# Attention weights made the stationary operand of "weights times values", with four tokens in column tiles, and the hand-over between four stages of a one-core layer rescheduled

## The reference

```python
q = (x @ wq.T + bq).reshape(B, S, 32, 16)      # k and v alike
scores = einsum('bshd,bstd->bsht', q, k) / 4   # 32 x 32 for each token
probs = softmax(scores, axis=-1)
context = einsum('bsht,bstd->bshd', probs, v).reshape(B, S, 512)
x = layernorm(x + context)
# feed-forward: w1, w2 (1376 x 512) and w3 (512 x 1376) are first quantised to the 16 values
# of NF4 in blocks of 64 (scaled by the block's largest magnitude) and dequantised
h = silu(x @ dq(w1).T) * (x @ dq(w2).T)
x = layernorm(x + h @ dq(w3).T)
```

## Time and profile before

| | |
|---|---|
| median of 3 runs | 812.72 us (812.71 to 813.48) |
| profiled execution, its own time | 811.45 us |
| span in the profile | 809.6 us |
| mean granted clock of TensorE | 0.847 |
| busy: PE, VectorE (DVE), ScalarE (ACT), POOL | 737.6, 630.4, 484.5, 102.6 us |
| DMA | 118.45 MB, mean 146 GB/s |

### The profile page before, as it was taken

The page is one execution under the profiler, slowest core; times in us unless marked ns, Lnnn a source line. Parts: engine busy times, 40 slices in busy tenths (PEclk is TensorE's granted clock), DMA queues, the critical chain, the costliest instruction groups (busy, mean ns, idle before and its releaser), DMA issues.

```text
span 809.6 us, 14305 instructions
## 1 busy us (share of the span) xinstructions
PE 737.6 (91%) x5688; PEld 629.3 (78%) x5688; DVE 630.4 (78%) x876; ACT 484.5 (60%) x650; POOL 102.6 (13%) x97
## 2 busy tenths in 40 slices
PE   5899999765899999999699999997999999899993
PEld 4778788654899999999587888885888888688761
DVE  2799999579888898987488998877787575965286
ACT  3688989384654636556554778674674546663124
POOL 2011101103000001010011111020111110100022
PEclk9999999975555655555699999998999999999995
DMA  9954444999987794963606260210415101340257
GB/s 221 232 159 156 148 155 157 257 243 259 234 214 189 226 262 135 278 157 133 232 1 203 85 210 26 81 54 26 141 30 171 45 4 35 118 148 12 104 157 155
DMA packets 89522, 118.45 MB, mean 146 GB/s; under 512 B 24784, under 2 KB 70864, under 8 KB 86512
## 3 DMA queue, kind: packets, MB, share of 16 engines
q1 hardware_dynamic: 88320, 115.44, 50.7%
q10 hardware_dynamic: 1136, 2.10, 1.2%
HBM read 76.42 MB, written 38.86 MB: 142 GB/s over the span
## 4 chain that ended last, share of the span: by engine, by line
PE 63%; DVE 12%; issue 9%; ACT 6%; DMA 4%; SPq 3%; POOL 1%; POOLq 0%; DVEq 0%; ACTq 0%
PE ps_p L1013 9%; PE ps_s L914 9%; PE ps_s L916 9%; PE ps_s L915 9%; PE ps_p L914 7%; PE ps_p L916 6%; PE ps_p L915 6%; DVE nf_acc L1136 4%; ACT nf_y L747 3%; PE ps_s L1000 3%; DMA qk_parts<-qk_p 2%; PE ps_t L952 1%; PE ps_t L938 1%; DMA k_st<-qk_parts 1%; SPq L408 1%
## 5 line engine op out<-in xcount | busy, mean ns | idle before, releaser
L1136 DVE SCALAR_TENSOR_TENSOR nf_acc<-nf_y,nf_acc 128x1024 f32<-128x1024 f32 (+4 forms) x266 | 303.3, 1140 | 32.5 <-ACT nf_y L747 23.6
L747 ACT ACTIVATE nf_y<-nf_w,bound_b 128x1024 f32<-128x1024 f32 (+4 forms) x285 | 288.9, 1047 | 9.7 <-DVE nf_acc L1136 4.0
L1013 PE MATMUL ps_p<-probT,v_bd 128*68 128x32 f32 x1024 | 125.6, 301 | 3.3 <-DVE probT L1185 3.3
L1013 PEld LDWEIGHTS ps_p<-probT,v_bd 128*68 128x68 f32 x1024 | 122.9, 211 | 4.4 <-issue 3.2
L1295 DVE TENSOR_TENSOR silu<-silu,ps_s 128x512 f32<-128x512 f32 (+1 forms) x44 | 30.2, 686 | 91.4 <-PE ps_s L916 91.2
L914 PE MATMUL ps_p<-x_hl,w_hl 128*128 128x512 f32 x192 | 78.8, 410 | 16.0 <-DVE qk_r L1160 10.3
L891 ACT ACTIVATE silu<-ps_s 128x512 f32<-128x512 f32 (+1 forms) x44 | 26.2, 596 | 95.6 <-PE ps_s L916 95.6
L668 POOL TENSOR_TENSOR nf_w<-nf_w,nf_rec 128x1024 f32<-128x1024 f32 (+4 forms) x19 | 39.7, 2089 | 335.4 <-DVE nf_rec L1120 335.4
L914 PE MATMUL ps_s<-x_hl,f_ha 128*128 128x512 f32 x192 | 76.1, 396 | 5.7 <-issue 5.7
L916 PE MATMUL ps_p<-x_hl,w_hl 128*128 128x512 f32 x192 | 76.7, 399 | 0.0
L915 PE MATMUL ps_p<-x_hl,w_hl 128*128 128x512 f32 x192 | 76.5, 399 | 0.0
(11 more groups left out here) (105 smaller groups left out, 1246.6 us busy)
## 6 DMA issues: line engine op xcount, KB each, us to landing
x_hl<-x_parts SPq DMA_DIRECT2D x10, 2048.0 KB, 8.9
qk_parts<-qk_p SPq DMA_DIRECT2D x64, 204.0 KB, 2.5
q_st<-qk_parts SPq DMA_DIRECT2D x48, 272.0 KB, 6.8
k_st<-qk_parts SPq DMA_DIRECT2D x48, 272.0 KB, 7.6
x_parts<-x_st SPq DMA_DIRECT2D x16, 512.0 KB, 3.8
nf_w<-in_L_ffn_w SPq DMA_DIRECT2D x24, 256.0 KB, 3.0
dequantised<-nf_acc SPq DMA_DIRECT2D x10, 512.0 KB, 4.4
v_blocks<-v_t SPq DMA_DIRECT2D x16, 256.0 KB, 3.0
```

The source lines that it names most:

```text
L747: act.activation(nf_y[0:p, at % NY, 0:w], nf_w[0:p, u % 2, 0:w], ACT.Identity, bias=bound_b[0:p, i:i + 1], scale=STEEP).then_inc(s_ny, 1)
L1013: t = pe.matmul(ps_p[0:MV, (G + 3) % NPV, i * H:(i + 1) * H], v_bd[hb % 2][:, :, g * GI + i], probT[:, G % 2, i], start=True, stop=True)
L1136: dve.scalar_tensor_tensor(out=acc, in0=y, scalar=float(NF4[i + 1]), in1=acc, op0=ALU.min, op1=ALU.max).then_inc(s_nacc, 1)
```

## The change

1. `values`: the softmax weights of one token (32 columns) are stationary, its block-diagonal values (68 columns) move. Four tokens are put side by side in the four column tiles of 32 PSUM partitions; the result of 16 such matmuls lies in [128, 4 x 68]. New: `evacuate` (ScalarE copies it to `ctmp`, three buffers) and `back` (four PE transposes bring it to [68, 512] in another PSUM bank), then `context` as before, a group later. Turns, moments and normalisation of a block come one group later.
2. First seam: the stack loads of half-block 0 are spread over three later slots, the value loads over a fourth; the last three slots of the projections have 1, 0, 0 levels instead of 2, 2, 2.
3. Second seam: x1 of the first block is loaded within the last group; the tail's turns use two more banks and another order of units; the last `back` and `context` come after the first gate and up chains.
4. Third and fourth seam: units are ordered first "w", both "t", other "w"; the levels per step change.

```diff
+        first = len(js) if g == 0 else 1
+        UNITS += [("w", g, j) for j in js[:first]] + [("t", g, t) for t in range(2)] + [("w", g, j) for j in js[first:]]
...
+    FIRST_STACKS = [FIRST_LOAD + 1 + 2 * k for k in range(3)]
+    FIRST_VALUES = FIRST_LOAD + 7
     LV_P = [1, 1, 1, 1, 1, 1, 1, 1, 2, 2, 2, 2] * NBK
+    LV_P[-3:] = [1, 0, 0]
...
-        LV_A[8 * b + 10:8 * b + 13] = [1, 1, 1]
+        LV_A[8 * b + 11:8 * b + 14] = [1, 1, 1]
...
-    LV_F = [(1, 2)] * 2 + [(1, 1)] * 2 + [(1, 2)] + [(2, 2)] * (FIRST_OF[2] - 5) + [(3, 4)] * 4 + [(3, 3)] * 2
+    LV_F = [(1, 2)] * 2 + [(1, 1)] * 2 + [(1, 0), (1, 2)] + [(2, 3)] * 20 + [(2, 2)] * 13
...
+    LATE = {8 * b + 8 + k: 8 * b + 14 + k // 2 for b in range(NBK - 1) for k in range(4)}
     for G in range(GG):
-        CONTEXT_AT.setdefault(max(G + 3, LATE.get(G, 0)), []).append(G)
+        CONTEXT_AT.setdefault(max(G + 4, LATE.get(G, 0)), []).append(G)
+        BACK_AT.setdefault(G + 4 if G % 8 == 2 and G > 8 else G + 3, []).append(G)
...
+    TAIL_1 = [("f", u, s) for u in (W_UNITS[0], T_UNITS[0]) for s in range(2)]
+    TAIL_2 = [("f", u, s) for u in (T_UNITS[1], W_UNITS[1]) for s in range(2)]
...
+    TAIL_S = (TAIL_1 + TAIL_2)[2:6]
+    def bank_of(n):
+        if n < NPT:
+            return n % 4
+        if TURNS[n] in TAIL_S:
+            return 2 + TAIL_S.index(TURNS[n]) % 2
+        return n % 2
...
+        ctmp = sb("ctmp", [P, NCT, 4 * MV], F32, att)
...
                     parts_stored(sp, 2 * KC)
-                    load_stacks(sp, 0)
+                if tau in FIRST_STACKS:
+                    load_stacks(sp, 0, [FIRST_STACKS.index(tau)])
+                if tau == FIRST_VALUES:
...
+                if G == GG - 1:
+                    load_x1(0)
...
+            def evacuate(G):
+                if G == 0:
+                    values_stored(act, KC * NBK)
+                act.wait_ge(s_pv, G + 1)
+                wait(act, s_back, G - NCT + 1)
+                act.activation(ctmp[:, G % NCT], ps_p[:, G % 2, 0:4 * MV], ACT.Copy).then_inc(s_evac, 1)
...
-                wait(pe, s_ctx, G - NPV + 1)
+                wait(pe, s_evac, G - 1)
                 for i in range(GI):
-                    t = pe.matmul(ps_p[0:MV, (G + 3) % NPV, i * H:(i + 1) * H], v_bd[hb % 2][:, :, g * GI + i],
-                                  probT[:, G % 2, i], start=True, stop=True)
+                    a, j = divmod(i, 4)
+                    t = pe.matmul(ps_p[32 * j:32 * j + 32, G % 2, a * MV:(a + 1) * MV], probT[:, G % 2, i],
+                                  v_bd[hb % 2][:, :, g * GI + i], start=True, stop=True)
                 t.then_inc(s_pv, 1)
+
+            def back(G):
+                pe.wait_ge(s_evac, G + 1)
+                wait(pe, s_ctx, G - 1)
+                for a in range(4):
+                    t = pe.transpose(ps_p[0:MV, 2 + G % 2, P * a:P * a + P], ctmp[:, G % NCT, a * MV:(a + 1) * MV],
+                                     ident[:])
+                t.then_inc(s_back, 1)
...
             for s in range(NS):
                 gate_up(s)
+                if s == 0:
+                    back(GG - 1)
```

More of the change, by code:

```diff
@@ L155, in layer_kernel @@
     HEADS = [range(0, 7), range(7, 14), range(14, 21), range(21, 28), range(28, 32)]
[L156 removed]
+    CT_AT, XT_AT, MOMENTS_AT, NORM_AT = {}, {}, {}, {}
     for b in range(NBK - 1):
         for k in range(len(HEADS)):
[L159 to L161 removed]
+            CT_AT.setdefault(8 * b + 11 + k // 2, []).append(("ct", b, k))
+        MOMENTS_AT[8 * b + 13] = b
+        NORM_AT[8 * b + 14] = b
         for c in range(KC):
[L163 to L166 removed]
+            XT_AT.setdefault(8 * b + 15 + c // 2, []).append(("xt", b, c))
+    BACK_AT, CONTEXT_AT = {}, {}
+    LATE = {8 * b + 8 + k: 8 * b + 14 + k // 2 for b in range(NBK - 1) for k in range(4)}
     for G in range(GG):
[L168 to L169 removed]
+        CONTEXT_AT.setdefault(max(G + 4, LATE.get(G, 0)), []).append(G)
+        BACK_AT.setdefault(G + 4 if G % 8 == 2 and G > 8 else G + 3, []).append(G)
+    for G in range(GG + 1):
         TURNS += CT_AT.get(G, []) + XT_AT.get(G, [])
@@ L208, in layer_kernel @@
     TURN = {key: n for n, key in enumerate(TURNS)}
+    TAIL_S = (TAIL_1 + TAIL_2)[2:6]
[5 more added lines that the diff above has]
+        return n % 2
+    EARLIER = {key: max((m for m in range(n) if bank_of(m) == bank_of(n)), default=-1) for key, n in TURN.items()}
     HIGH = {key: n for n, key in enumerate(k for k in TURNS if k[0] != "ct")}
@@ L273, in layer_kernel @@
         f3_la = sb("f3_la", [P, NJG, E], F32R)
+        x1_hl_0 = sb("x1_hl0", [P, 2, KC, BK], F32R)
         f3_ha = sb("f3_ha", [P, NJG, E], F32R)
         f1_ha = sb("f1_ha", [P, 2, KC, NJG * P], F32R)
-        x1_hl = [sb(f"x1_hl{i}", [P, 2, KC, BK], F32R) for i in range(2)]
+        x1_hl = (x1_hl_0, sb("x1_hl1", [P, 2, KC, BK], F32R))
         hid_hl = sb("hid_hl", [P, 2, 2, BK], F32R)
@@ L321, in layer_kernel @@
         s_pv = sem("s_pv")
+        s_evac = sem("s_evac")
+        s_back = sem("s_back")
         s_ctx = sem("s_ctx")
@@ L400, in down_over, with load_stacks @@
                 eng.wait_ge(s_down, step + 1 - n)
-        def load_stacks(eng, hb):
-            for b in range(3):
+        def load_stacks(eng, hb, which=range(3)):
+            for b in which:
                 for i, terms in enumerate((Q_TERMS, K_TERMS)):
@@ L424, in turn_bank @@
         def turn_bank(key):
[L425 to L428, removed]
+            n = bank_of(TURN[key])
+            return (ps_t, ps_s)[n // 2][:, n % 2]
         def turn_shape(key):
@@ L522, in load_v, with store_x1, load_x1 @@
                                  ).then_inc(s_ldv[hb % 2], 16)
+            def store_x1(key):
+                _, b, c = key
+                low_done(sp, key)
+                sp.dma_start(x1_d[b, :, :, c], x1_st[:, c % 2].bitcast(F32)).then_inc(s_stx[c % 2], 16)
+            def load_x1(n):
+                b = ORDER[n][1]
+                if n == 0:
+                    sp.wait_ge(s_pv, GG - NG)
+                elif n == 1:
+                    sp.wait_ge(s_score, GG)
+                else:
+                    sp.wait_ge(s_up, LAST_STEP[max(k for k in range(n) if ORDER[k][1] == (b + 2) % NBK)] + 1)
+                x1_stored(sp, b)
+                sp.dma_start(x1_hl[b % 2][:].bitcast(F32), x1_d[b]).then_inc(s_ldx[b % 2], 16)
             for q in range(2):
@@ L599, in _ @@
                         reload(u)
+                if G == GG - 1:
+                    load_x1(0)
                 for key in XT_AT.get(G, []):
[L601 to L612, removed]
+                    store_x1(key)
+            for key in XT_AT.get(GG, []):
+                store_x1(key)
             def store_out(n, q):
@@ L861, in _ @@
                     context(at)
+                if G >= 3:
+                    evacuate(G - 3)
                 steep(LV_A[G] // 2)
@@ L868, in _ @@
                 steep(LV_A[G] - LV_A[G] // 2)
+            context(GG - 4)
+            evacuate(GG - 3)
+            for key in XT_AT.get(GG, []) + TAIL_1:
+                high(key)
+            evacuate(GG - 2)
             context(GG - 3)
-            for key in TAIL_1:
-                high(key)
-            context(GG - 2)
             steep(LV_T[0])
@@ L875, in _ @@
                 high(key)
-            context(GG - 1)
+            evacuate(GG - 1)
+            context(GG - 2)
             steep(LV_T[1])
@@ L891, in _ @@
                 act.activation(silu[0:rows, s % 2], ps_s[0:rows, 0], ACT.Silu).then_inc(s_silu, 1)
+                if s == 0:
+                    context(GG - 1)
                 steep(LV_F[s][0])
@@ L918, in turn @@
             def turn(key):
[L919 to L923, removed]
+                if EARLIER[key] >= 0:
+                    low_done(pe, TURNS[EARLIER[key]])
+                if key in TAIL_S[:2]:
+                    pe.wait_ge(s_ssub, GG)
                 kind, k, c = key
@@ L1078, in _ @@
                     values(G - 2)
+                for at in BACK_AT.get(G, []):
+                    back(at)
                 for key in XT_AT.get(G, []):
@@ L1081, in _ @@
             values(GG - 2)
-            for key in TAIL_1:
+            for key in XT_AT.get(GG, []) + TAIL_1:
                 turn(key)
+            back(GG - 3)
             values(GG - 1)
@@ L1086, in _ @@
                 turn(key)
+            back(GG - 2)
             pe.wait_ge(s_minus_i, 1)
```

21 lines of the change are left out of this document (8 added, 13 removed).

## The result

| | before | after |
|---|---|---|
| median, us | 813.1 (4 runs, 812.71 to 813.76) | 834.05 (4 runs, 831.39 to 836.3) |
| profiled execution: time / span | 811.45 / 809.6 | 834.1 / 832.3 |
| VectorE busy / ScalarE busy | 630.4 / 484.5 | 681.6 / 508.1 |

The ratio is 1.0256 [1.0224, 1.0287]: 21 us slower, where 26 us faster was predicted.

A forecast was written before the change was run, and what follows sets the result against it. TensorE and the VectorE-ScalarE loop were taken as level, the real losses as TensorE's idle seams. Terms -11.5 - 2.2 - 2.5 - 13.0 + 3 = -26.2 took 811.45 to 785.3, plus 1.3 for the median: 786 us; 8 in 10: 777 to 803.

The forecast's parts named there:

- The step that failed: Attention, steady state: TensorE's group falls to 4.1 us, under the VectorE-ScalarE loop, so little shows: -2.2 us.
- the 4.79: Attention: us a plain group takes in the VectorE-ScalarE loop of shift, exp, pass and lifts, read from the profile before.
- the range that I gave for TensorE's group: Attention: TensorE's group of scores, new product and transposes was put at 4.1 us, between 3.2 and 4.9.
- the sum: Whole kernel: all terms together, -26.2 us, giving 786 us; chance of 780 to 790 us 0.50.
- The product's 1.94 us: Attention, values: a token's second pass overlaps only the next token's first, so 16 x 121 ns a group.
- The lower bound of 1.0: Attention, values: with four column tiles wholly abreast the product takes 3.89/4 = 1.0 us a group.
- tiles in series: Rival, attention values: column tiles don't overlap, 813 us or up to about 905; chance 0.05 near no change, 0.08 clearly slower.
- ScalarE's evacuation: Attention: the added copy takes some 0.4 us a group (0.3 to 0.57), hidden in 1.56 us idle before exp.
- First seam, -11.5: Projections to attention: spread loads remove the 10.3 us store wait and group 4 starts earlier; -11.5 us, bounds 6 and 15.
- Second seam, -2.5: Attention to feed-forward: earlier x1 load and two more banks for the turns; -2.5 us, bounds 0 and -5.
- Third, fourth and the lifts, -13.0 + 3 = -10: Feed-forward: reordered units and fewer late lifts remove idle stretches, -13.0 us; extra lifts in steps 6 to 25 cost +3.
- the VectorE-bound rival: Rival, feed-forward steps 6 to 25: VectorE becomes the bound, +12 us in place of +3, 795 us; chance 0.20.

The follow-up runs named there:

- e1: The changed kernel with the old weights-times-values product, context read and order of turns, so the seams alone: 798.23 us, 0.9814 to the kernel before.
- e6: e1 with the values' rows padded to 272 bytes and three value buffers: 802.71 us, 0.9897 to the kernel before.
- e11: The changed kernel with 272-byte rows, without evacuations and transposes back, in the old order of turns: 796.31 us, 0.9798 to the kernel before.
- e8: e5 (272 bytes) with the stores of the first two x1 tiles issued ahead of the twelve stack loads: 800.86 us, 0.9854 to the kernel before.
- e5: The whole changed kernel with values' rows padded to 272 or 260 bytes and three value buffers: 804.56 us (272), 804.79 us (260).
- e3: The changed kernel with each product reading 68 consecutive numbers of the values' tile, not 68 standing 256 bytes apart: 803.12 us, 0.9879 to the kernel before.
- e9: The kernel before with the first seam alone, five lifts moved to the feed-forward: 809.28 us, 0.9959 to the kernel before.

## Why the prediction was wrong, step by step

**The step that failed** is in the attention: "TensorE's group becomes 1.28 + 1.94 + 0.88 = 4.1 ... under the 4.79 of the VectorE-ScalarE loop ... -2.2". The group did become short, and TensorE is off the loop. But the step took the 4.79 as a property of VectorE and ScalarE, fixed whatever TensorE does beside them. With four column tiles reading at 256 bytes it isn't: 6.2 us. I bounded the new matmul's own duration from both sides and never its effect on the neighbours. (Nor is the range that I gave for TensorE's group below the loop throughout, as I wrote: its upper end, 4.9, lies above 4.79.) Put together from the ratios, in a chain from e1 to the change: e1 to e6 +6.7 us, e6 to e11 -8.0, e11 to e8 +4.6, e8 to e5 +4.9, e5 (272) to the change +27.8. The last is the disturbance, less what the cure costs (the first step says little of that, since it holds the slower load of the old product). e3, which has neither the padding nor one buffer less, lies 30.6 us below the change (1.0256 to 0.9879). So the disturbance is 28 to 31 us. The rest of the step's forecast failed too, on a smaller scale: with the disturbance and the late stores cured (e8, 0.9854), the new product still brings no gain over the seams alone (0.9814), where the sum had 2.2 us.

**The product's 1.94 us** was hit (1.99 to 2.06), by a wrong argument, and that is luck. Tiles of different tokens do overlap nearly wholly: 3.92 us with one tile, 1.20 with four when the rows are 272 bytes. At 256 bytes it is 2 us, and the same edit that shortens it frees the neighbours; that its reads queue there is my reading of this, not measured. The lower bound of 1.0 was nearly right, and the rival "tiles in series" wrong in its mechanism; the side on which it stood came from elsewhere.

**ScalarE's evacuation**: 0.38 us as predicted, and hidden in the groups, as e8 and e11 show. With the transposes and the moved turns it costs 4.6 us all the same, behind group 31, none of which the sum had. The sum credited the pair of x1 turns that leaves the loop for the tail and did not charge the tail with it: in e8 ScalarE waits there 1.55 and 1.74 us for stores before the pair's two copies. No run separates the pair from the evacuations and the transposes. *Moved stores*: the sum counted SP's queue at the first seam and not at x1's turns. They cost 4.9 us in e5; in the change itself the same groups take 7.59 and 7.48 us, where e5 has 10.25 and 9.50, so less of it shows.

**First seam, -11.5**: the wait in the last projections went and scores(4) came at 195.93, ended by a DMA, a little past the 190 to 195 of the prediction. But the term measured -3.3 alone (e9) and about -5 on top of the later seams; the feed-forward, into which the five lifts moved, takes 2.8 us longer in e9 (the sum had that in its +3), and the -3.3 is net of it. Two things were missing. First, with five lifts fewer the next unit starts later, and its weights are then issued behind the twelve stack loads: at 187.33 (landed 196.81), where before they went ahead of them, at 176.34 (landed 179.60). VectorE waits 3.63 us for them ahead of group 4 (199.41 in place of the predicted 193.5), 4.53 in e9. Second, 5.3 us of e9's lead are given back by group 31. VectorE does the same work in that stretch (27 groups, 42 lifts, three units begun), but waits for scores 5.8 us in nine waits, from group 7 to group 28, where before it was 1.3 in three: 4.5 of the 5.3. The two longest, 1.64 and 1.32, are at groups 7 and 11, the latter with turns of the context beside it (above). Why TensorE is late there more often than before stays open.

**Second seam, -2.5**: in e1 from group 31 to the first gate matmul it is 19.8 us, 24.1 before: -4.3, inside the bounds. In the change it is 24.8, and with the disturbance cured (e8) still 23.4: the tail has the moved pair of turns and the last transposes back (above). **Third, fourth and the lifts, -13.0 + 3 = -10**: measured -8.8 in the change, -8.3 in e1, and TensorE's waits for VectorE in steps 6 to 25 are at most 1.2 us; the VectorE-bound rival is not what happened. The later seams alone give 9.7 us against a predicted 12.5.

With the product left out, the sum's other terms, -24.0, met 15.1.

## What to carry to other kernels

Price an instruction not only by its own duration but by what it does to those beside it: look in the trace for the same operation of VectorE or ScalarE with and without the new TensorE work at its side. When four column tiles read an f32 moving operand at a distance of 256 bytes, give the rows a few unused numbers (or one); that was worth 28 us here. Other powers of two were not run. When a transfer is moved, or work that a transfer waits for, look up what its queue issues ahead of it in the new place: both x1's stores and the unit's weights fell behind twelve stack loads.

## What was not expected of the hardware

- Matmuls of f32 in four column tiles with a moving operand of 68 numbers at 256 bytes' distance stretch what VectorE, ScalarE and GpSimd do in SBUF by about 1.3 us in 2 us, at the most 1.9 (a pass 1.19 to 2.52 and once 3.05, a shift 0.65 to 2.02, a normalisation 2.01 to 3.28). The Trainium skill ("SBUF — State Buffer", Who interferes with whom) says that TensorE and ScalarE never wait on anyone; the 2.52 us pass of ScalarE speaks against it.
- At 272 or 260 bytes, at consecutive numbers, or in one or two tiles, there is next to none of it. The same page (Door 1: The DMA port swizzle, the paragraph on cachelines) has each access that leaves a line of 16 bytes pay a penalty. By that 272 bytes would be no better than 256; here the product took 1.20 against 1.99 us, and 1.13 with consecutive numbers. The measurement decides: with four tiles at once it is 256 bytes that costs, and 260 or 272 hardly do. Which part of the memory the reads meet in stays open.
- As weights, the same rows behave the other way: 3.94 us a group at 256 bytes, 4.25 at 272. This stays unexplained.
